# Fourteen experts, two to a token: whole quads through every expert, or rows sorted into tiles of one expert

## The reference, cut to what matters

```python
# x: the tokens, normalised (mean and variance over the 128 features)
scores = softmax(x @ gate_w.T)                 # 14 per token
top2, idx = top_k(scores, 2)                   # the two best
top2 = top2 / max(sum(top2), 1e-10)
y_e = gelu(x @ w1[e] + b1[e]) @ w2[e] + b2[e]  # 128 -> 256 -> 128
out = x_normalised + sum_k top2[k] * y_idx[k]
x   = x + clip(out, -100, 100)
```

## Time and profile before

| | |
|---|---|
| median of three runs | 1635.33 us |
| the profiled execution | 1631.55 us |
| its span, first to last instruction | 1629.7 us |
| TensorE busy | 1456.6 us (89%), mean granted clock 0.964 |
| VectorE busy | 1180.9 us (72%) |
| ScalarE busy | 899.3 us (55%) |
| GpSimd busy | 728.6 us (45%) |
| DMA | 18.99 MB |

### The profile page before, as it was taken

The page is one execution under the profiler, slowest core; times in us unless marked ns, Lnnn a source line. Parts: engine busy times, 40 slices in busy tenths (PEclk is TensorE's granted clock), DMA queues, the critical chain, the costliest instruction groups (busy, mean ns, idle before and its releaser), DMA issues. The chain is left out here.

```text
span 1629.7 us, 28961 instructions
## 1 busy us (share of the span) xinstructions
PE 1456.6 (89%) x10026; PEld 938.0 (58%) x10026; DVE 1180.9 (72%) x2570; ACT 899.3 (55%) x2614; POOL 728.6 (45%) x694
## 2 busy tenths in 40 slices
PE   5998887899799999998898988999977887899998
PEld 3665554555577765553343326888864443577776
DVE  5888567689687766548899897777767889754443
ACT  3675332377677752227776765777752444454442
POOL 4557454222664441328888894333351334451000
PEclk9999998999999999999999999999997998999999
DMA  7000000000000000020000000000000000000000
GB/s 304 1 2 1 1 1 1 1 2 2 2 1 2 2 1 1 1 93 0 1 1 1 0 1 1 2 1 2 2 2 0 1 0 1 1 1 7 7 7 7
DMA packets 3168, 18.99 MB, mean 12 GB/s; under 512 B 592, under 2 KB 720, under 8 KB 2256
## 3 DMA queue, kind: packets, MB, share of 16 engines
q1 hardware_dynamic: 3024, 17.14, 2.6%
HBM read 16.09 MB, written 1.05 MB: 11 GB/s over the span
## 5 line engine op out<-in xcount | busy, mean ns | idle before, releaser
L835 POOL TENSOR_TENSOR l_xattn_probs<-l_xattn_probs,l_xattn_recip 128x512 f32<-128x512 f32 x128 | 133.1, 1040 | 220.2 <-DVE l_xattn_recip L774 219.7
L1032 ACT ACTIVATE l_attn_probs<-ps,l_attn_neg_max 128x128 f32<-128x128 f32 x512 | 145.0, 385 | 69.2 <-DVE l_attn_neg_max L1094 69.1
L2750 POOL TENSOR_TENSOR l_mamba_hc<-l_mamba_h,l_mamba_c 128x512 f32<-128x512 f32 x128 | 159.0, 1269 | 0.0
L2671 DVE TENSOR_TENSOR_SCAN l_mamba_h<-ps,l_mamba_dBx 128x512 f32<-128x512 f32 x128 | 152.6, 1212 | 1.8 <-ACT ps L2568 0.7
L2444 PE MATMUL ps<-l_mamba_hc,w_const 128*128 128x512 f32 x256 | 136.4, 638 | 19.2 <-POOL l_mamba_hc L2750 16.5
L3428 DVE SCALAR_TENSOR_TENSOR xn<-ps,l_gates,xn 128x128 f32<-128x128 f32 x224 | 63.1, 344 | 108.7 <-PE ps L3065 107.9
L769 DVE COPY l_xattn_probsT<-ps 128x512 f32<-128x512 f32 x128 | 87.9, 687 | 69.9 <-PE ps L621 69.9
L3202 ACT ACTIVATE wkv<-ps,w_early 128x512 f32<-128x512 f32 x112 | 70.8, 683 | 110.4 <-PE ps L3054 110.3
L3065 PEld LDWEIGHTS ps<-w_early,wkv 128*128 128x128 f32 x896 | 107.5, 192 | 21.5 <-issue 18.9
L720 ACT ACTIVATE l_xattn_probs<-ps,l_xattn_neg_max 128x128 f32<-128x128 f32 x256 | 91.7, 388 | 41.5 <-DVE l_xattn_neg_max L764 41.5
L245 POOL TENSOR_TENSOR rs<-rs,neg_half 128x4 f32<-128x4 f32 (+2 forms) x32 | 43.4, 1357 | 157.1 <-DVE rs L239 157.0
(11 more groups left out here) (526 smaller groups left out, 3635.0 us busy)
## 6 DMA issues: line engine op xcount, KB each, us to landing
w_early<-in_l_moe SPq DMA_DIRECT2D x1, 3669.0 KB, 12.4
w_l_xattn<-in_l_xattn SPq DMA_DIRECT2D x1, 2176.0 KB, 18.7
w_early<-in_l_xattn SPq DMA_DIRECT2D x1, 1890.0 KB, 11.7
w_l_attn<-in_l_attn SPq DMA_DIRECT2D x1, 1242.0 KB, 22.4
ctx<-in_ctx SPq DMA_DIRECT2D x1, 1088.0 KB, 7.1
x<-in_x SPq DMA_DIRECT2D x2, 512.0 KB, 5.1
ctxT<-in_ctxT SPq DMA_DIRECT2D x1, 1024.0 KB, 4.8
out_x<-x SPq DMA_DIRECT2D x4, 256.0 KB, 2.3
```

The source lines that it names most:

```text
L835: nc.gpsimd.tensor_tensor(probs[:, D % 2, n, :, :], probs[:, D % 2, n, :, :], along(recip[:, D % 2, n, :], [P, HALF, P]), ALU.mult).then_i ...
L1032: ins = nc.scalar.activation(probs[:, t % 4, g, :], S_of(t)[:, g * P:(g + 1) * P], ACT.Exp, bias=neg_max[:, t % 2, g:g + 1], accum_out=total)
L2671: nc.vector.tensor_tensor_scan(flat(h[:, t % 2, half, :, :]), G.ps[:, DA_BANK[half], :], flat(dBx[:, t % 2, half, :, :]), 0.0, ALU.mult, A ...
L2750: nc.gpsimd.tensor_tensor(heads4(hc[:, t % 4, half, :]), h[:, t % 2, half, :, :], c_sb[:, t % 3, :, :], ALU.mult).then_inc((hc0_set, hc1_s ...
```

## The change

A quad's 1024 choices (512 tokens, two each) are sorted by expert into tiles of 128 rows, and each tile goes through one expert alone. There are 21 tiles a quad: tile e < 14 belongs to expert e and holds its first 128 rows, and seven more tiles (`MORE`) are handed out to experts with more than 128 rows. All 21 are always worked on.

- `best_two` also writes the choices in bf16 (`picks`) and splits them into a first and a second choice (`which`). TensorE's `rank` counts, with a triangular and an all-ones matrix in bf16, how many rows of each expert come at or before a token. `place` makes from that a row number for each choice (`places`) and the experts of the seven extra tiles (`owners`).
- `scatter(q)` on GpSimd: eight indirect DMAs, each of 128 rows of 512 B from the normalised tokens to their places in DRAM (`sorted_in`). SyncE loads the 21 tiles back (`load_rows`, three DMAs) and the weights of the seven extra tiles with addresses from registers (`load_chosen`, seven DMAs of 264 KB).
- `turn_rows` transposes groups of up to four tiles, VectorE copies them (`copy_rows`). `first(n)` and `second(n)` now work on pairs of tiles, 11 pairs a quad (the last of one tile), four products each of 128 columns; `gelu(n)` is four activations of 128x128; VectorE copies four tiles of results (`copy_y`), SyncE stores them to DRAM (`store_results`, three DMAs).
- `fetch(q)` on GpSimd: eight indirect DMAs bring each token's two results back, `combine(q)` on VectorE adds weight times result, two for each block, in place of the fourteen gathers.
- The four DRAM buffers `sorted_in` are filled with zeros at the start of the function (four DMAs of 1.4 MB), after a memset on GpSimd; ScalarE waits for them before the attention of layer 3.
- The choice for quad 0 moves into the attention of quad 3: turn_tokens(0) and rate(0) into attend(LAST), and on VectorE below_max(0), received_spreads(1), best_two(0) and place(0) ahead of the scans 2 and 3. The normals of quads 1 to 3 move from GpSimd to VectorE.
- Buffers for rows and results reuse those of the attention (`large`, `wide`), which ties the first load to the end of it.

The diff, cut to its core:

```diff
-    "l3_moe": dict(gate=(128, 14), w1=(128, 3584), b1=(128, 28), w2=(128, 3584), b2=(14, 128)),
+    "l3_moe": dict(gate=(128, 14), experts=(128, 7196), b2=(14, 128), first_row=(128, 14), jump=(128, 14),
+                   over=(128, 3), turn=(128, 7)),
...
+        FIXED, MORE, X = 14, 7, EC * P + EC * D + EC
+        TILES, GROUPS, PAIRS = FIXED + MORE, 6, 11
...
+            def load_rows(q):
+                sp.wait_ge(scattered, 16 * 2 * QUAD * (q + 1))
+                after(sp, rows_up, GROUPS * (q - 1))
+                if q == 0:
+                    sp.wait_ge(o_set, CH * NQ)
+                    sp.wait_ge(s_made, NQ)
...
+            load_rows(0)
+            load_chosen(0)
+            for q in range(NQ):
+                store_results(q, 0)
+                if q + 1 < NQ:
+                    load_rows(q + 1)
+                store_results(q, 1)
+                store_results(q, 2)
+                if q + 1 < NQ:
+                    load_chosen(q + 1)
+                if q > 0:
+                    store(q - 1)
+            store(LAST)
...
+            rank(0)
+            turn_gates(0)
+            turn_tokens(1)
+            rate(1)
+            add_biases(0)
+            turn_rows(0)
+            turn_rows(1)
+            first(0)
+            first(1)
+            for j in range(QUAD):
+                project(LAST, j)
+            rank(1)
+            turn_gates(1)
+            for n in range(PAIRS * NQ):
+                second(n)
+                if n + 3 in begun_at:
+                    turn_rows(begun_at[n + 3])
+                if n + 2 < PAIRS * NQ:
+                    first(n + 2)
+                if n in (10, 20):
+                    turn_tokens(n // 10 + 1)
+                if n in (12, 22):
+                    rate(n // 10 + 1)
+                if n in (16, 25):
+                    rank(n // 10 + 1)
+                if n in (18, 27):
+                    turn_gates(n // 10 + 1)
+                if n in (8, 25, 29):
+                    add_biases({8: 1, 25: 2, 29: 3}[n])
...
+            for n in range(PAIRS * NQ):
+                gelu(n)
+                if n == 1:
+                    take_out(LAST)
+                    take_gates(1)
+                if n == 3:
+                    receptance(LAST - 1)
+                if n == 9:
+                    receptance(LAST)
+                if n in (12, 22):
+                    take_tokens(n // 10 + 1)
+                if n in (14, 24):
+                    exponentials(n // 10 + 1)
+                if n in (20, 28):
+                    take_gates((n + 2) // 10)
...
+            def combine(q):
+                dve.wait_ge(fetched_set, 16 * 2 * QUAD * (q + 1))
                 dve.wait_ge(biased, q + 1)
+                for k in range(2):
+                    for j in range(QUAD):
+                        b = q * QUAD + j
+                        nc.vector.scalar_tensor_tensor(G.xn[:, b, :], fetched[:, q % 2, k, j, :], weight[:, q, k, j:j + 1], G.xn[:, b, :],
+                                                       ALU.mult, ALU.add).then_inc(summed, 1)
+                    dve.wait_ge(summed, QUAD * (2 * q + k + 1))
...
+            for n in range(PAIRS * NQ):
+                if n + 3 in begun_at:
+                    copy_rows(begun_at[n + 3])
...
+                if n == 15:
+                    best_two(2)
+                    weights_of(2)
+                if n == 17:
+                    place(2)
+                if n == 20:
+                    combine(0)
+                    close(0)
...
+                if n in ended_at:
+                    copy_y(ended_at[n])
...
+            def scatter(q):
+                pool.wait_ge(placed, q + 1)
+                pool.wait_ge(m_normed, QUAD * (q + 1))
+                if q == 0:
+                    pool.wait_ge(empty, 16 * NQ)
+                for k in range(2):
+                    for j in range(QUAD):
+                        nc.gpsimd.indirect_dma_start(sorted_in[q], bass.IndirectOffsetOnAxis(ap=places[:, q, k, j:j + 1], axis=0),
+                                                     G.xn[:, q * QUAD + j, :], None).then_inc(scattered, 16)
...
             shifts(LAST - 1)
             out_scale(LAST)
+            receive(LAST - 1)
             add_out(LAST)
+            received_normals(2)
             shifts(LAST)
-            receive(LAST - 1)
             receive(LAST)
-            received_normals(LAST - 1)
-            received_normals(LAST)
+            received_normals(3)
+            scatter(2)
+            fetch(0)
+            scatter(3)
+            fetch(1)
+            fetch(2)
+            fetch(3)
```

More of the change, by code:

```diff
@@ new lines, in rank, with turn_rows @@
+                mm.then_inc(ranked, 1)
+            def turn_rows(gg):
+                q, g = gg // GROUPS, gg % GROUPS
+                pe.wait_ge(rows_loaded[g > 0], 16 * (1 if g == 0 else 2) * (q + 1))
+                after(pe, rows_copied, gg - 1)
+                if gg < 2:
+                    pe.wait_ge(v_set, CH * NQ)
+                for j, t in enumerate(tiles_in(g)):
+                    mm = nc.tensor.transpose(G.ps[:, R_BANK[gg % 2], j * P:(j + 1) * P], rows[:, q % 2, t, :], G.c["ident"])
+                mm.then_inc(rows_up, 1)
@@ L3487, in _ @@
                     stats(q - 1)
+                    below_max(0)
+                    received_spreads(1)
                 if f == LAST:
@@ L3493, in _ @@
                 scan(q, 1)
+                if q == LAST:
+                    best_two(0)
+                    weights_of(0)
+                    received_here(1)
+                    place(0)
                 if f < LAST:
@@ new lines, in _ @@
+            best_two(1)
+            weights_of(1)
+            copy_rows(0)
+            copy_rows(1)
+            place(1)
+            take_biases(0)
+            for n in range(PAIRS * NQ):
+                if n + 3 in begun_at:
+                    copy_rows(begun_at[n + 3])
+                if n == 2:
+                    attended_spreads(2)
+                if n == 3:
+                    stats(LAST)
+                if n == 5:
+                    apply(LAST)
+                if n == 7:
+                    received_spreads(2)
+                if n == 8:
+                    attended_spreads(3)
+                if n == 9:
+                    received_here(2)
+                    take_biases(1)
+                if n == 13:
+                    received_spreads(3)
+                    below_max(2)
+                if n == 14:
+                    received_here(3)
+                if n == 15:
[6 more added lines that the diff above has]
+                    close(0)
+                if n == 26:
+                    take_biases(2)
+                if n == 23:
+                    below_max(3)
+                if n == 24:
+                    best_two(3)
+                    weights_of(3)
+                if n == 27:
+                    place(3)
+                if n == 33:
+                    take_biases(3)
+                if n == 31:
+                    combine(1)
+                    close(1)
+                if n == 42:
+                    combine(2)
+                    close(2)
+                if n in ended_at:
+                    copy_y(ended_at[n])
```

318 lines of the change are left out of this document (200 added, 118 removed).

## The result

The changed kernel takes 1642.7 us in the median of 20 runs (1637.2 to 1648.9), the kernel before 1635.2 in the same session; the ratio is 1.0035, 95% interval [1.002, 1.005]. So the change makes the kernel slower by about a third of a per cent, where the forecast was 1623 us and faster. The profiled execution of the changed kernel has a span of 1639.7 us.

A forecast was written before the change was run, and what follows sets the result against it. TensorE's matmul count was taken to bound the experts' stage. After the change, opening, middle, last quad and tail summed to 1612.8 us; 5 for the clock gave span 1618, and 5.6 up to the median 1623.6, given as 1623; range 1592 to 1654.

The forecast's parts named there:

- the price that decides: Cost d of each of 64 indirect DMAs on GpSimd: taken as 0.9 us, bounds 0.20 to 1.81, 48 in the sum.
- Rival (2): GpSimd's queue takes over, d over 1.1; not faster from 1.16, 1641 us at 1.27, 1667 at 1.81; chance 0.30.
- T0: Start of second(0), put at 1456.5 us; Tn likewise means the start of second(n), the second layer of pair n.
- the clock: TensorE restarts at a lower clock after stalls: some 2 us lost each, 5 us in all (0 to 10).
- The removed work: Experts' stage: TensorE loses 112 us of work, 84 tiles take 84.3 us, a pair is taken as 2.05.
- The opening: VectorE's choices ahead of the first pair: first(0) at about 1443 us against 1411.3 before, second(0) at 1456.5.
- The middle: From second(0) to second(33): waits for scatters, fetches and combine; second(4) at 1470.0, second(22) at 1532.1, second(33) at 1572.5.
- The tail: After the last copy at 1594.9 us, uncovered store, fetch(3), landing, combine and close; end at 1612.8.
- Covered at no cost: Zero-fill hidden by 18 us of cover, memset costing at most 1 us, chosen weights' 6.3 us load under 14 us of pairs.
- Rival (4): Chosen experts' tiles or loads come late; at 20 us a load, each quad waits 6, giving 1647 us; chance 0.08.
- The page: Skill page calling descriptor generation small, 2.0 us fixed completion cost; states the cheap-issue rival, d 0.2 to 0.7, 1589 to 1613, chance 0.20.
- the middle case: Whole-kernel time within 8 us of the kernel before, d of 1.0 to 1.33; chance 0.21.

The follow-up runs named there:

- The head turned round: Changed kernel with place(1) ahead of the weights and two copies, rank(1) and last projections ahead of the first pair: 1632.6 us, ratio 0.9967.
- the combination with the stores moved: Changed kernel with later additions (combine(0) at pair 29), place(1), rank(1) and last projections sooner, SyncE's stores a quad later: 1632.7 us, ratio 0.9985.

## Why the prediction was wrong

**The step that failed** is the price that decides: d, the time from one indirect DMA on GpSimd to the next, was taken as 0.9 from rows of 0.78 and 1.03 and is 1.26. The sum holds it 48 times, 48 x 0.36 = 17.3 us, and with d at 1.26 the prediction's own formula gives 1640.3; 1642.7 was measured. That it comes so near is partly luck: for the span the same sum gives 1635.3 and 1639.7 was measured, and the difference is no more than the 4.3 us ahead of the sublayer (below) that this execution happened to have. Rival (2) is what happened, at its value for d of 1.27 (1641), and its threshold of 1.16 was passed. GpSimd isn't full, though (78 us busy of 199): its issues stand in one chain with VectorE's choice, the loads and combine. The busy part was taken almost rightly (0.96); what was missed is the gap of 0.30 between two such instructions that wait for nothing. That the issues are on the path is shown, not only read: with 24 of them and 12 products left out the stretch from T0 on is 26.4 us shorter, and the scatters of the middle and the fetch of the tail give back their full price. For the fetches of the middle it is shown in part only. Their landing was put at 2.3 us, measures 3.4, and grew to 6.3 when fewer were issued, so there a smaller d would have been partly eaten up by the landing.

Where the changed kernel's profile and the prediction's milestones part (the unchanged work ahead of the sublayer happened to end 4.3 us later in this execution, 1220.01 against 1215.67 for the sublayer's first row on VectorE):

| stretch | predicted | measured | difference |
|---|---|---|---|
| up to T0 | 1456.5 | 1463.4 | +6.9, 4.3 of them ahead of the sublayer |
| T0 to T4 | 13.5 | 15.5 | +2.0 (8 x 0.36 = 2.9) |
| T4 to T10 | 15.9 | 19.9 | +4.0 |
| T10 to T15 | 14.7 | 13.6 | -1.1 |
| T15 to T22 | 31.5 | 37.2 | +5.7 (16 x 0.36 = 5.8) |
| T22 to T33 | 40.4 | 47.3 | +6.9 (5.8) |
| T33 to the end | 40.3 | 42.9 | +2.6 (2.9) |

The differences are 27.0 us: 17.3 for d, 4.3 ahead of the sublayer, and 5.4 for the rest, for which the clock had been given 5 in a lump. The stretches that hold a d are off by it and by little else. The stretch from T4 to T10 holds none and is off by 4.0; no run says why.

**The removed work** was sized rightly: the tiles' count, and the pair step of 2.05 us. In the last quad TensorE does two pairs in 4.0 us. ScalarE doesn't pace them.

**The opening** missed a wait. turn_rows(1) stands ahead of first(0) and waits 3.7 us for the second and third load of the rows; the third lands 4.8 us behind the first. The load was taken as one of 2.3, and its three parts take 3.0, 4.7 and 6.7 in the median. first(0) came at 1452.2, 4.9 later than predicted even beside the later start. Half was made good: T0 is off by 2.6. The head turned round is the remedy for that place, worth 10 us alone (8 in the trace).

**The middle** held in form. From T15 to scatter(2) it is 10.42 us (1512.36 to 1522.78) and was predicted 10.5. combine waits for the fetch and holds copy_y, as said, and the experiment that moves it away gave 15.7 us. The rows of quad 2 come earlier than that wait ends, as said too: TensorE idles 13.0 us for the rows, does two pairs, and idles 5.9 more for copy_y, 18.9 where 17 was said for d of 0.9. Two signs came out otherwise. Ahead of pair 33 TensorE idles 11.9 us (6.1 and 5.8) instead of 19; from T22 to T33 it is busy 31.5 us at a granted clock of 0.83, where the prediction had 21.5 free of waits. And VectorE's waits in combine(0) and combine(1) are 6.3 and 6.5 us, not 10 to 20, since VectorE first waits 14.3 and 9.4 us for turned rows in copy_rows; its longest wait for a DMA is in combine(3), 14.2.

**The tail** was predicted 17.9 from the last copy's end to the end of the span and took 20.4 (from 1618.40 + 0.88), 2.5 more, where d alone would give 2.9. The last quad ahead of it took 22.5 against 22.4.

**Covered at no cost**: the fill's four transfers landed after 8.9 us and nobody waited for them; the memset had been said to cost at most 1 us. It held VectorE by more: an instruction of 1.08 us in the kernel before takes 3.50, and that stretch of VectorE is 2.3 us longer (8.0 and 5.8). Whether that reaches the end isn't shown, since the run that moved the memset only moved the wait. Rival (4) didn't come: no engine waits for the chosen experts' weights in the trace.

**The page.** The Trainium skill's page DMA: Bandwidth & Descriptors, section Anatomy of one DMA (SWDGE path), calls descriptor generation small; the trace disagrees, at 0.96 us busy and 1.26 from start to start for 128 rows, and the measurement decides. Its fixed cost of about 2.0 us fits a scatter's 2.2 from issue to landing. As a rival it would have given under 1613.

The chances were put with 0.53 on faster. By the prediction's own bounds the result is the middle case (within 8 us, d of 1.0 to 1.33), which had 0.21; it held that one couldn't tell this from none, and twenty runs of each kernel do (interval 1.002 to 1.005). d's bounds, 0.20 and 1.81, were wide, and its point was chosen by nearness to two instructions of other kinds; no row of the trace before spoke strongly for one side of 1.16.

## What to carry to other kernels

Count what a sparse scheme puts into a serial queue, not only what it takes from the wide engine: here TensorE's 112 us less work, by count, was bought with 48 indirect DMAs at 1.26 us each in the chain, 60 us, with the landings, the orders that stand behind them and a lower clock on top. Where a change adds one unseen instruction many times on the path, work out first the price at which the sign turns, and measure that price before the rest. Look also at what runs beside a transfer: the same fetch landed in 2.5 us alone and in up to 6.2 beside the row loads. And put a wait for a gather where its data have arrived: moving two additions by 8 pairs turned this change from a loss of 0.35% into a gain of 0.5%.

## What the runs showed of the hardware

**A small VectorE instruction can last as long as a run of GpSimd's.** VectorE's cast of 128x56, with the GpSimd instructions beside it:

```profile
1440.43 4.20 DVE L3549 CAST l_picks<-l_gates 128x56 bf16<-128x56 f32 x1
```

```profile
1440.87 2.48 POOL L3786 TENSOR_TENSOR l_wide<-l_state,l_wide 128x512 f32<-128x512 f32 x2
1443.31 1.26 POOL L3795 TENSOR_TENSOR l_out<-l_out,w_l_attn 128x512 f32<-128x512 f32 x1
```

The cast ends at 1444.63, GpSimd's third operation at 1444.57; alone such a cast takes 0.2 us. Likewise L3400, a tensor_scalar of 128x32, lasts 3.50 us up to 1224.23, when the third of GpSimd's memsets in a row ends (1224.19). The Trainium skill, page SBUF — State Buffer, section Who interferes with whom, says that the two engines share a port pair that one holds for a whole instruction; the trace agrees, and adds that the loser may stay out over three back-to-back instructions. The same section tells of VectorE starving descriptor generation on GpSimd; here the indirect DMAs kept to 0.94 to 1.07 us beside VectorE's work, but for the first two of the kernel (1.25 and 1.43), and no run shows why these were longer.

**Indirect DMAs cost the same in both directions**, 0.96 (scatter) and 0.94 us (fetch). A scatter's landing takes 2.2 us in the median. A fetch's takes 2.4 to 2.6 in the tail, alone, and 2.6 to 6.2 beside the loads of rows (fetch(0)).

**The clock.** With TensorE at 121 us of work in 199, its granted clock is 0.79, and eight matmuls behind a stall take 2.04 to 2.08 us instead of 1.06. The clock takes a part of what a thinner load saves.

**An unexplained stall** of TensorE in the third or fourth quad, 7 us and more in the combination with the stores moved, in all versions measured in the later sessions and in none of the earlier, as told above.
